# Streaming the next image's tiles through a ring of eight, and shortening the lag of the quantised convolution, in the last two layers of a four-layer convolution kernel

## What is computed

```python
x = x + _L0_conv_ref(_gn(x), L0_conv_w, L0_conv_b)
x = x + _L1_conv_ref(_gn(x), L1_conv_w_real, L1_conv_w_imag, L1_conv_b_real, L1_conv_b_imag)
x = x + _L2_conv_ref(_gn(x), L2_conv_weight_int8, L2_conv_scale_weight, L2_conv_bias)
x = x + _L3_conv_ref(_gn(x), L3_conv_weight)
```

```python
x_q = jnp.round(jnp.clip(x_cl / scale_input, -n, n))
acc = lax.conv_general_dilated(x_q, w_hwio, window_strides=(1, 1), padding=((1, 1), (1, 1)), ...)
out = acc * (scale_input * scale_weight) + bias
```

## Time and profile before

| | us |
|---|---|
| median of 3 runs | 6229.66 |
| lowest, highest | 6224.24, 6241.02 |
| the profiled execution | 6232.09 |
| its span on the core | 6230.2 |
| granted TensorE clock, mean | 0.949 |

### The profile page before, as it was taken

The page is one execution under the profiler, slowest core; times in us unless marked ns, Lnnn a source line. Parts: engine busy times, 40 slices in busy tenths (PEclk is TensorE's granted clock), DMA queues, the critical chain, the costliest instruction groups (busy, mean ns, idle before and its releaser), DMA issues. The chain is left out here.

```text
span 6230.2 us, 202732 instructions
## 1 busy us (share of the span) xinstructions
PE 5335.2 (86%) x63882; PEld 3402.6 (55%) x63882; DVE 5053.6 (81%) x10660; ACT 4538.9 (73%) x8793; POOL 3153.6 (51%) x5676
## 2 busy tenths in 40 slices
PE   0379979979979979979989989968898988989889
PEld 0058748748748748747757757833343433434334
DVE  5879979979979989988998998986676766767664
ACT  2578768868868867867876666768787877878775
POOL 3178768758858858858857858921111110111102
PEclk9889989989989989999999999989999999999999
DMA  6516616616616625625624524646676766767665
GB/s 203 158 47 209 204 40 206 207 46 201 206 53 190 208 69 171 208 88 159 206 95 115 159 84 113 177 94 155 166 204 163 204 162 159 200 162 196 168 163 139
DMA packets 535621, 958.88 MB, mean 154 GB/s; under 512 B 121946, under 2 KB 126938, under 8 KB 532826
## 3 DMA queue, kind: packets, MB, share of 16 engines
q1 hardware_dynamic: 467546, 798.95, 45.0%
q10 hardware_dynamic: 67456, 151.01, 7.8%
HBM read 560.40 MB, written 287.60 MB: 136 GB/s over the span
## 5 line engine op out<-in xcount | busy, mean ns | idle before, releaser
L1655 PE MATMUL pC<-xs,taps 128*128 128x512 f16 x4608 | 1095.8, 383 | 106.7 <-DMA xhalo<-xs 100.4
L981 PE MATMUL pM<-gw,xh 64*128 64x256 f16 (+1 forms) x24960 | 1130.7, 244 | 5.5 <-DVE yt L1141 4.7
L981 PEld LDWEIGHTS pM<-gw,xh 64*128 64x128 f16 x24960 | 972.5, 95 | 133.4 <-issue 12.0
L1551 POOL TENSOR_TENSOR xn<-xn,one_col 128x1 f32<-128x1 f32 x520 | 170.4, 328 | 1406.4 <-ACT xn L1585 1406.4
L1655 PEld LDWEIGHTS pC<-xs,taps 128*128 128x128 f16 x4608 | 449.3, 98 | 672.1 <-DVE xs L1705 90.2
L1571 ACT ACTIVATE scaled<-X,qbias,qscale 128x512 f32 (+1 forms) x512 | 413.3, 808 | 327.8 <-DMA X<-after_layer 297.0
L742 POOL TENSOR_TENSOR X<-X,zo 128x256 f32 (+1 forms) x512 | 372.5, 727 | 548.3 <-DVE zo L1105 548.3
L279 PE MATMUL pM<-X,mix0s 64*64 64x512 f32 x2304 | 530.1, 634 | 134.5 <-DVE X L1073 108.5
L723 POOL TENSOR_TENSOR X<-X,rl 128x512 f32 x384 | 478.4, 1275 | 270.8 <-ACT rl L772 270.7
L1593 ACT ACTIVATE xs<-xn 128x1028 f16<-128x1028 f32 x520 | 546.8, 1051 | 86.7 <-POOL xn L1552 86.2
L1712 DVE SCALAR_TENSOR_TENSOR result<-pC,X 128x512 f32<-128x512 f32 x512 | 352.4, 688 | 303.3 <-DMA out_dram<-result 181.4
(11 more groups left out here) (249 smaller groups left out, 13574.2 us busy)
## 6 DMA issues: line engine op xcount, KB each, us to landing
gw<-row_weights SPq DMA_DIRECT2D x520, 288.0 KB, 3.4
after_layer<-X SPq DMA_DIRECT2D x512, 256.0 KB
out_dram<-result SPq DMA_DIRECT2D x512, 256.0 KB
X<-in_x_dram SPq DMA_DIRECT2D x448, 256.0 KB
X<-after_layer ACTq DMA_DIRECT2D x224, 512.0 KB, 5.7
stage<-in_x_dram SPq DMA_DIRECT2D x192, 512.0 KB
xhalo<-xs SPq DMA_DIRECT2D x504, 96.4 KB, 3.7
qhalo<-q SPq DMA_DIRECT2D x496, 96.2 KB, 3.9
```

The lines of the kernel that those rows point to most:

```text
L981: nc.tensor.matmul(pY[:, r, col:col + nd * P], row(xh, r)[:, k, p, ri, off:off + P], weights(r, q_, d, nd, ri), start=ri == 0 and off == 1 ...
L1655: nc.tensor.matmul(bank, taps3[:, d, wh], xs[:, h, own, d:d + W], start=d == 0 and n == 0, stop=False)
```

## The change

`DELAY` goes from 12 to 8, and the loop is 78 turns long instead of 83. The slot numbers of c2's rings, which depended on t through DELAY, are now computed by `second(k, g)`. In detail:

- The tiles of image b + 1 no longer go to `Xf` by a transfer of two tiles that ACT issues. SP issues one transfer of 256 KB for each tile into `stream`, a ring of eight tiles in SBUF, at turn t for tile t - 5, three turns ahead of its `scale2`. It waits until `update` of the tile eight places before has read the slot, and that `update` stands in the same turn on DVE.
- `scale2` and `update` read `stream` (for image 0 they still read `Xf`). `update` writes `Xf`, and waits for the store of the tile that image b had there.
- `finish` writes in place to `Xf` instead of to `result`, without a wait for a store, and `store` reads `Xf`. SP now waits for the store of four tiles before ahead of each store.
- SP's order in a turn was halos, then store. It is now load, store, halos.
- `conv2` lags four turns behind `scale2` instead of five, `update` five instead of six and `square3` six instead of seven. So in turn t ACT scales tile t - 8, PE convolves tile t - 12, and DVE updates tile t - 13.
- `scaled` has two buffers instead of four. `square3` throws its result into a single PSUM bank instead of two bf16 tiles in SBUF. The row of zeros for the image's border is read from DRAM instead of from an SBUF tile.

```diff
-        DELAY = 12
+        DELAY = 8
+        AHEAD = 12
...
-                scaled = sb("scaled", [P, 4, W], f32, pm)
-                unused = sb("unused2", [P, 2, W], mybir.dt.bfloat16, pm)
+                scaled = sb("scaled", [P, 2, W], f32, pm)
+                stream = sb("stream", [P, RING, W], f32, pm)
...
-                result = sb("result", [P, 4, W], f32, pm)
...
+                unused = ps("unused2", [P, W], pm)
...
+                def second(k, g):
+
+                    n = k + AHEAD - DELAY
+                    return n % RING, g + n // RING
...
+                    def store(b, v, k, g):
 
                         tile, slot = v - 1, (k - 9) % 4
+                        n = tile // 4 if isinstance(tile, int) else 2 * g - 3 + (k + 3) // 4
+                        wait_alone(sp, out_stored[slot], (b * (J // 4) + n + 1) * 16, passed)
                         sp.wait_ge(x4_ready, b * J + v)
...
+                    def load(b, w, k):
+
+                        slot = (k - 1) % RING
+                        wait_alone(sp, x3_ready, b * J + w - 7, passed)
+                        sp.dma_start(stream[:, slot], x2s[b].rearrange("(j s) c w -> (s c) j w", s=BANDS)[:, w]).then_inc(loaded2[slot], 16)
 
                     def both(b, c3, c2):
                         def step(t, k, g):
+                            k2, g2 = second(k, g)
+                            if c3 and c2 and live(t, DELAY - 3, DELAY - 3 + J):
+                                load(b + 1, t - DELAY + 3, k2)
+                            if c3 and live(t, 9, J + 9):
+                                store(b, t - 8, k, g)
                             if c2 and k % 2 == 0 and live(t, DELAY, DELAY + J + 1):
-                                halos2(b + 1, t - DELAY, k)
+                                halos2(b + 1, t - DELAY, k2)
                             if c3 and k % 2 == 1 and live(t, 1, J + 2):
                                 halos3(b, t, k)
-                            if c3 and live(t, 9, J + 9):
-                                store(b, t - 8, k)
...
-                            if c3 and c2 and k % 2 == 0 and live(t, 10, J + 10):
-                                load(b + 1, t - 10, k, g)
-                            if c2 and live(u, 7, J + 7):
-                                square3(b + 1, u - 7, k)
+                            if c2 and live(u, 6, J + 6):
+                                square3(b + 1, u - 6, k2)
...
-                            w, v = t - DELAY - 5, t - 6
+                            w, v = t - DELAY - 4, t - 6
...
-                    def update(b, w, k):
+                    def update(b, w, k, g, first):
                         dve.wait_ge(conv2_done, b * J + w + 1 + CONV2_CREDIT)
...
+                        if not first:
+                            n = w // 4 if isinstance(w, int) else 2 * g - 5 + (k + 3) // 4
+                            dve.wait_ge(out_stored[(k - 1) % 4], ((b - 1) * (J // 4) + n + 2) * 16)
```

More of the change, by code:

```diff
@@ L1564, in _, with scale2 @@
                 def _(act):
[L1565 to L1571 removed]
+                    def scale2(b, w, k, g, first):
+                        slot = (k + 4) % RING
+                        if not first:
+                            n = w // RING if isinstance(w, int) else g - 2 + (k + 4) // RING
+                            wait_alone(act, loaded2[slot], ((b - 1) * (J // RING) + n + 1) * 16, passed)
+                        if not (isinstance(w, int) and w < 2):
+                            wait_alone(act, q_ready, b * J + w - 1, passed)
+                        nc.scalar.activation(scaled[:, k % 2], Xf[:, w] if first else stream[:, slot], ACT.Identity, bias=qbias[:, bass.ds(b, 1)],
                                              scale=qscale[:, bass.ds(b, 1)]).then_inc(scaled_ready, 1)
                     def square3(b, j, k):
[L1575 removed]
+                        act.wait_ge(sq3_done, b * J + j + 2)
                         act.wait_ge(x3_ready, b * J + j + 1)
[L1577 removed]
+                        nc.scalar.activation(unused[:, :], Xf[:, j], ACT.Square, bias=bias2[:, :],
                                              accum_out=sq3[:, bass.ds(j, 1)]).then_inc(sq3_done, 1)
@@ L1605, in step @@
                             u = t - DELAY
+                            k2, g2 = second(k, g)
                             if c2 and live(u, 0, J):
-                                scale2(b + 1, u, k, g)
+                                scale2(b + 1, u, k2, g2, not c3)
                             if c3 and live(t, 1, ITEMS + 1):
@@ L1693, in quant @@
                         dve.wait_ge(conv2_done, b * J + w + 1)
-                        nc.vector.tensor_scalar(q[:, (k + 5) % RING, 1:W + 1], scaled[:, k % 4], MAGIC, -MAGIC, ALU.add,
+                        nc.vector.tensor_scalar(q[:, (k + 5) % RING, 1:W + 1], scaled[:, k % 2], MAGIC, -MAGIC, ALU.add,
                                                 ALU.add).then_inc(q_ready, 1)
-                    def update(b, w, k):
+                    def update(b, w, k, g, first):
                         dve.wait_ge(conv2_done, b * J + w + 1 + CONV2_CREDIT)
-                        nc.vector.scalar_tensor_tensor(out=Xf[:, w], in0=pC2[:, (k - 2) % 4], scalar=oscale2[:, :], in1=Xf[:, w],
+                        if not first:
+                            n = w // 4 if isinstance(w, int) else 2 * g - 5 + (k + 3) // 4
+                            dve.wait_ge(out_stored[(k - 1) % 4], ((b - 1) * (J // 4) + n + 2) * 16)
+                        nc.vector.scalar_tensor_tensor(out=Xf[:, w], in0=pC2[:, (k - 1) % 4], scalar=oscale2[:, :],
+                                                       in1=Xf[:, w] if first else stream[:, (k - 1) % RING],
                                                        op0=ALU.mult, op1=ALU.add,
@@ L1717, in step @@
                             u, v = t - DELAY, t - 7
+                            k2, g2 = second(k, g)
                             if c3 and live(v, 1, J + 1):
-                                finish(b, v, k, g)
-                            if c2 and live(u, 6, J + 6):
-                                update(b + 1, u - 6, k)
+                                finish(b, v, k)
+                            if c2 and live(u, 5, J + 5):
+                                update(b + 1, u - 5, k2, g2, not c3)
                             if c2 and live(u, 0, J):
-                                clip(b + 1, u, k)
+                                clip(b + 1, u, k2)
                             if c3 and live(t, 1, ITEMS + 1):
```

56 lines of the change are left out of this document (18 added, 38 removed).

## The result

| | before | after |
|---|---|---|
| median, lowest, highest (us) | 6235.34, 6224.24, 6242.60 (4 runs) | 6346.24, 6341.25, 6348.28 (4 runs) |
| span of the profiled execution | 6230.2 | 6342.4 |
| granted TensorE clock, mean | 0.949 | 0.949 |

The changed kernel takes 1.0176 times as long (95% interval 1.0161 to 1.0191), 1.8% more. The forecast was 6350 us.

A forecast was written before the change was run, and what follows sets the result against it. PE was taken to bound the stretch with both convolutions, then the halo chain after the change. Seven image periods of 274.1 us against 259.5 (+102) and the run-in (+18) raised 6232.1 to 6352, median 6350 us; range 6165 to 6460.

The forecast's parts named there:

- SP's place ahead of the halos: Turns with both layers: load and store delay the halos past PE's pace, 3.925 us a turn, 231.6 us for 59 tiles.
- S: The moment when PE begins an even turn t in the last stage; halos were forecast issued at S + 3.82.
- `conv3` alone: Part of an image before `conv2` joins: loses five tiles, gains 2.65 us for first halos, 17.4 us from 29.7.
- `conv2` alone: Image's end after the last `conv3`: five tiles left instead of ten, 9.5 us instead of 19.4.
- Run-in: Image 0 of the last stage: the bare halo chain takes 3.58 us a pair instead of 2.94, +18 us.
- The parts priced at nothing: Loads and store waits in part three, and ACT's `scaled` and `square3` changes: hidden behind PE, no cost.
- PE's wait for `qhalo`: Sign in mid-image: grows from 76 us to 150 to 250, mostly once in two turns, about 0.9 us each.
- PE's busy share of the stretch: Sign in the part with both convolutions: should fall to about 88%.
- The one that the chain fits: Faster rival: halos land in 3.0 us or less, PE stays the bound, 6168 us; chance 0.18.
- the cancelling rival: No change: break-even at 3.64 us a turn or 3.4 us landing; halos right behind `quant` just match PE; chance 0.09.
- The slow rival: Halos wait for writes ahead, landing 5.0 us, about 6560 us; decides from about 4.45 us on; chance 0.11.
- The rule behind it: A semaphore increment lands only after all earlier writes of that DMA engine, so halos wait for store and load ahead.

The follow-up runs named there:

- e3_before_lag4: The kernel before with only `conv2` four turns behind its scaling instead of five, update five, square six: 6272.60 us, ratio 1.0055.
- e5_before_buffers: The kernel before with only two `scaled` buffers instead of four and `square3`'s result in one PSUM bank: 6228.50 us, ratio 0.9987.
- e4_act_loads: The changed kernel with the 256 KB loads issued by ACT behind `square3`, two turns ahead, instead of SP; lag four kept: 6254.78 us, ratio 1.0037.
- e1_lag5: The changed kernel with `conv2` five turns behind its scaling again, loads on SP two turns ahead: 6221.22 us, ratio 0.9986.
- e14_sp_waits5: The kernel of e9_act_lag5 plus five already satisfied waits a turn on SP, no data moved: 6173.90 us, ratio 0.9917.
- e6_lag5_first: The changed kernel with lag five and SP's order halos, load, store, loads on SP: 6328.48 us, ratio 1.0157.
- e9_act_lag5: The changed kernel with loads issued by ACT two turns ahead and `conv2` five turns behind its scaling: 6149.39 us, ratio 0.9866.
- e10_lag3: The changed kernel with `conv2` three turns behind `scale2` instead of four: 7643.22 us, ratio 1.2265.

## Why the prediction was right, point by point

The sum against the profiled executions: I had 6232 + 102 + 18 = 6352 us, and the execution took 6344.2. The terms:

- **SP's place ahead of the halos, the step on which the forecast rested: right, a little too large.** I had the halos issued at S + 3.82, a landing of 3.95 and a turn of 3.925 us. In the pair shown they are issued at S + 3.37 and `conv2` starts at S + 7.78; in the median of all pairs they are issued at S + 3.2. The issue of a load is 0.34 us on SP and not 0.66, the figure of the other stage's loads, whose access pattern is another. The landing is 4.1 us in the median, and `conv2` starts 0.26 us after it, where I had 0.05. The mean turn is 3.844 us: 59 x 0.081 x 7 = 33 us less than I had. So the halos went out earlier than I had them, and what follows took longer; the two misses cancel in part within this term.
- **`conv3` alone: the term most under-sized.** I had 17.4 us, with 2.65 us for the first halos; it is 19.4 us. About half of the miss is that I started from one image with 29.7 us, where the mean of the kernel before is 30.8. The rest is the wait for the first halos, 3.4 to 5.1 us and 4.3 in the mean, where I had 0.7 + 2.65. 7 x 2.0 = 14 us more than I had. Behind this wait 7 to 13 matmuls run at the lower clock (1.46 instead of 0.81 us for three). The forecast had no such term; it is some 2 us an image and is counted in the turns above.
- **`conv2` alone:** 9.5 us predicted, 9.7 measured. The statistics' own term and the first 13 us are as before.
- **Run-in:** +18 us predicted, +21.8 measured, and e3_before_lag4 shows that the lag alone does it.
- **Before the stage, 7.0 us:** DVE's first instruction of the last stage starts at 4111.63 us instead of 4104.60. The code there is the same, and the executions of the experiments have it between 4097.9 and 4119.8 us. This is the spread from one execution to the next, and no part of the change.
- **The parts priced at nothing** (ACT's loads, `finish` without its wait, `scaled`, `unused`) cost nothing, by the waits above and e5_before_buffers.

Together -33 + 14 + 3.8 + 7 give -8, the difference between 6352 and 6344; the small terms sum to less than 1. The prediction's errors cancelled in part, so that it lies within 4 us of the median is luck. The mechanism and the direction are not: the mean pair of turns is 7.7 us for a forecast 7.85, the end of an image 9.7 for 9.5, and the run-in grew by 21.8 us for 18.

Of what I said would show: PE's wait for `qhalo` is 138 us where I had 150 to 250 (with the zero row's 24 us it is 162). It is 0.93 us in the mean, as said; in the stretches with both layers it comes 133 times in 206 pairs of turns, not in every pair. The halos follow `quant` by 0.84 us, as said. PE's busy share of the stretch is 94% and not 88%. The shorter turn makes it 90% (3.47 of 3.844 us). The rest is in how the rows count: matmuls at half clock are busy, and the record of the last matmul before a wait reaches 0.16 us further than its turn (0.81 us for three of 0.217).

**The rivals.** The one that the chain fits needed a landing of 3.0 us or less; the median was 4.1. But e4_act_loads and e3_before_lag4 show that the chain of four turns comes close to fitting in the middle of an image (3.625 and 3.595 us) once SP adds nothing, as the text on the cancelling rival says of halos right behind `quant`. The slow rival needed 4.45 us or more. The rule behind it, from the section "Queues, rings and completion order" of the Trainium skill's page "DMA: Bandwidth & Descriptors", would have the halos seen only after the store that was issued 0.86 us ahead of them. The medians from 4239 us on are 3.9 to 4.4 us where the last store was issued 0.8 to 1.0 us ahead on the same queue (4.1 in after, 4.2 in e1_lag5, 4.4 in e14_sp_waits5). Where it was issued further ahead they are 3.4 to 4.3 us: 3.4 in e6_lag5_first (1.5 us ahead), 4.2 in e9_act_lag5 (1.8), 3.9 in e4_act_loads (2.1), 3.7 in e3_before_lag4 (2.4) and 4.2 before (2.7). In the run-in, without loads and stores, it is 2.7 us. So beside this traffic the landing is 0.7 to 1.7 us longer, but it does not follow the store's distance: the rule's wait, if it was there, was short here. The load ahead can't be it in any case, since it has landed 3.0 us after its issue in the median (line 1530), and so before the halos.

What the forecast did not see is that SP's queue, and not only the place in it, is nearly full with four transfers a turn. It counted SP's time ahead of one transfer and never added up SP's whole turn.

## What to carry to other kernels

Add up the whole turn of the engine that issues the DMAs, waits and gaps included, as one does for the others: here a load cost SP 0.34 us of issue and 0.46 us of gap, and that took SP's turn to PE's. Of a transfer that is moved, ask first what it is put ahead of, and what the load's own wait makes it stand behind: the same load was free on ACT, cost 72 us on SP ahead of the halos, and 179 us behind them, all with the lag of five. And a chain that fits in steady state can still cost where nothing else hides it, as the run-in and the first `conv2` of an image show.

## What the runs showed of the hardware

- A wait that is already satisfied, with its counter increment, takes about 0.15 us of SP (three of them +0.48 us in the gap, nine +1.26), and it moves no data.
- The issue of a 256 KB load from DRAM to SBUF took 0.34 us on SP, on ACT's queue as well, while a 256 KB store took 0.74 and each halo transfer of 96 KB about 0.6. The issue time doesn't follow the bytes.
- After PE had been idle for 4.1 us its matmuls took 0.42 instead of 0.217 us for thirteen matmuls (1.2 instead of 2.4 GHz), which made the wait in e10_lag3 cost 6.6 us and not 4.1. After waits of 3.4 to 5.1 us in after, 7 to 13 matmuls took that long.
- 96 KB from SBUF to SBUF land in 2.7 us without other traffic, and in 3.4 to 4.4 us, by the medians of all kernels here, beside a load and a store of 256 KB a turn. The median does not follow how far ahead the last store was issued (0.8 to 2.9 us). Why e6_lag5_first lies lowest is not known.
